# A macaron block on one core: normalisation 3 moves to ScalarE, and four small edits to the routing

## What is computed

```python
x = x + 0.5 * ffn(layernorm(x))
x = x + mixer(layernorm(x))
x = x + 0.5 * ffn(layernorm(x))

# mixer: proj = x @ W_in.T, gate and value halves; depthwise convolution with 5 taps on the value;
# u = sigmoid(gate) * (conv + bias); recurrence h = tanh(a) * h + u over time; res = x + h @ W_out.T;
# the result is layernorm(res) * ln_w + ln_b

# ffn: 32 experts of width 64, 4 chosen for each token, and one shared expert of width 128
scores = sigmoid(tokens @ router_weight.T)
sfc = scores + router_bias
group_scores = top_k(sfc in 4 groups of 8, 2).sum()
keep = the 2 groups with the highest group_scores      # others: sfc := 0
topk_idx = top_k(masked sfc, 4)
topk_w = scores[topk_idx] / (sum + 1e-20) * 2.5
out = sum over chosen of topk_w * (silu(x @ gate.T) * (x @ up.T)) @ down.T  + shared expert
```

## Time and profile before

| | before |
|---|---|
| median of three runs | 779.44 us (778.56 to 781.64) |
| the profiled execution | 780.84 us, span 779.0 us |
| TensorE busy | 737.8 us, 95% |
| VectorE busy | 625.7 us, 80% |
| GpSimd busy | 506.4 us, 65% |
| ScalarE busy | 421.6 us, 54% |
| mean granted clock of TensorE | 0.972 of full speed |

### The profile page before, as it was taken

One profiled execution on the slowest core, in us unless ns is written; L12 is line 12 of the kernel. 1 busy time (PEld: TensorE's weight loads), 2 busy tenths in 40 slices (PEclk: granted clock), 3 DMA queues, 4 the chain that ended last, 5 costly groups with the idle time before them and its releaser, 6 DMA issues. The chain is left out here.

```text
span 779.0 us, 12555 instructions
## 1 busy us (share of the span) xinstructions
PE 737.8 (95%) x3320; PEld 591.0 (76%) x3320; DVE 625.7 (80%) x1719; ACT 421.6 (54%) x777; POOL 506.4 (65%) x716
## 2 busy tenths in 40 slices
PE   6799968899999999999999999999999999988896
PEld 5587756687888788887888788887888788766685
DVE  5887767798789979798789979798789978767853
ACT  4444634365656556565656556565656555544453
POOL 3255754467866777567866787567865786665465
PEclk9799978999999999999999999999999999998999
DMA  7200000000000000000000000000000000000000
GB/s 193 53 0 2 14 0 1 17 11 0 16 1 28 2 1 13 14 14 1 14 0 27 0 1 13 11 17 1 14 0 13 0 0 15 1 0 1 0 14 14
DMA packets 22868, 10.53 MB, mean 14 GB/s; under 512 B 5376, under 2 KB 22816, under 8 KB 22816
## 3 DMA queue, kind: packets, MB, share of 16 engines
q1 hardware_dynamic: 22288, 9.74, 4.5%
q10 hardware_dynamic: 528, 0.26, 0.1%
HBM read 7.90 MB, written 2.10 MB: 13 GB/s over the span
## 5 line engine op out<-in xcount | busy, mean ns | idle before, releaser
L400 POOL TENSOR_TENSOR hid_lo<-hid,hid_hi 128x256 fp32r<-128x256 f32 x544 | 411.3, 778 | 221.6 <-ACT hid_hi L517 220.8
L517 ACT ACTIVATE hid_hi<-hid 128x512 fp32r<-128x512 f32 x272 | 171.1, 629 | 150.1 <-DVE hid L670 125.6
L655 DVE TENSOR_TENSOR weighted<-silu_sb,wb_ps 128x512 f32<-128x512 f32 x256 | 174.4, 681 | 78.2 <-ACT silu_sb L508 44.7
L508 ACT ACTIVATE silu_sb<-gate_ps 128x512 f32<-128x512 f32 x272 | 161.3, 593 | 128.0 <-PE gate_ps L943 126.6
L670 DVE TENSOR_TENSOR hid<-weighted,up_ps 128x512 f32<-128x512 f32 x256 | 174.2, 681 | 13.9 <-DVE weighted L655 1.9
L1006 PE MATMUL down_ps<-hid_lo,wt_hi 128*128 128x512 f32 x272 | 109.1, 401 | 4.2 <-POOL hid_lo L400 4.2
L1003 PE MATMUL down_ps<-hid_hi,wt_hi 128*128 128x512 f32 x272 | 109.8, 404 | 1.5 <-ACT hid_hi L517 1.5
L1004 PE MATMUL down_ps<-hid_hi,wt_lo 128*128 128x512 f32 x272 | 108.6, 399 | 0.0
L941 PE MATMUL gate_ps<-xT_hi,wt_hi 128*128 128x512 f32 x238 | 100.0, 420 | 1.9 <-issue 1.9
L963 PE MATMUL wb_ps<-wT,pick 128*128 128x512 f32 x256 | 100.5, 403 | 0.1
L941 PE MATMUL up_ps<-xT_hi,wt_hi 128*128 128x512 f32 x238 | 95.7, 402 | 2.0 <-DVE hid L670 1.2
(11 more groups left out here) (150 smaller groups left out, 1074.2 us busy)
## 6 DMA issues: line engine op xcount, KB each, us to landing
x_res<-in_L_attn_x SPq DMA_DIRECT2D x8, 256.0 KB, 2.8
out_x<-x SPq DMA_DIRECT2D x8, 256.0 KB, 2.3
x_ln<-in_L_attn_x SPq DMA_DIRECT2D x7, 256.0 KB, 3.0
raw<-in_L_ffn_gate_w SPq DMA_DIRECT2D x4, 256.0 KB, 5.8
raw<-in_L_ffn_up_w SPq DMA_DIRECT2D x4, 256.0 KB, 5.0
raw<-in_L_ffn_down_w SPq DMA_DIRECT2D x4, 256.0 KB, 5.0
x_ln<-in_L_attn_x ACTq DMA_DIRECT2D x1, 256.0 KB, 6.9
raw<-in_L_attn_W_in SPq DMA_DIRECT2D x1, 128.0 KB, 2.7
```

The lines of the kernel that those rows point to most:

```text
L400: last = nc.gpsimd.tensor_tensor(hid_lo[s][:, cols], hid[s][:, cols], hid_hi[s][:, cols].bitcast(F32), ALU.subtract)
L508: nc.scalar.activation(silu_sb[s][:, :], gate_ps[s][:, :], ACT.Silu).then_inc(silu_done, 1)
L517: nc.scalar.activation(hid_hi[s][:, :], hid[s][:, :], ACT.Copy).then_inc(hid_hi_done, 1)
L655: V.tensor_tensor(weighted[s][:, :], silu_sb[s][:, :], wb_ps[j % 2][:, :], ALU.mult)\
```

## The change

Four edits, all in how VectorE's small work is done:

1. The application of normalisation 3 goes from VectorE (four operations, slot 1.5 of a tail unit, slot 10 of a double unit) to ScalarE, which calls `normalise` with `res` as its source, in slot 1 of a tail unit and slot 10 of a double unit, in each behind the silu of that slot and the high part of the tile before. `scaled` and x2 keep their slots.
2. The group differences are made by one operation over all four token groups instead of four.
3. The group mask is an int32 of -1 or 0 (the comparison is multiplied by -1), the masked scores are the bitwise AND of scores and mask, and the addition of 0.0 is gone.
4. `chosen` has a 33rd column, set once to 1e-20, so that the sum over it contains the addition of 1e-20, which is gone. `ROUTE`, the number of counted steps of a routing, goes from 32 to 30.

```diff
-        TAIL = {"meanvar 3": 0, "norm 3": 0, "normalise 3": 1.5, "scale 3": 2, "x2": 3, "stats 4": 3.5,
+        TAIL = {"meanvar 3": 0, "norm 3": 0, "normalise 3": 1, "scale 3": 2, "x2": 3, "stats 4": 3.5,
...
-        ROUTE = 32
+        ROUTE = 30
...
@@ scalar: unit, behind hidden_high(*main, j - 1)
+                    if j == steps.get("normalise 3"):
+                        normalise(3, chain if tail is None else tail, res)
...
@@ vector: route_part
                 if part == 4:
                     st.wait()
-                    for t in range(TT):
-                        last = V.tensor_tensor(gdiff[:, t, :].rearrange("p (g h) -> p g h", g=NG),
-                                               gsum[:, t, :].unsqueeze(1).broadcast_to([P, NG, NG]),
-                                               gsum[:, t, :].unsqueeze(2).broadcast_to([P, NG, NG]), ALU.subtract)
-                    st.done(last)
+                    st.done(V.tensor_tensor(gdiff[:, :, :].rearrange("p t (g h) -> p t g h", g=NG),
+                                            gsum[:, :, :].unsqueeze(2).broadcast_to([P, TT, NG, NG]),
+                                            gsum[:, :, :].unsqueeze(3).broadcast_to([P, TT, NG, NG]),
+                                            ALU.subtract))
...
-                    st.done(V.tensor_scalar(gmask[:, :], grank[:, :], float(GTOP), None, ALU.is_lt))
+                    st.done(V.tensor_scalar(gmask[:, :], grank[:, :], float(GTOP), -1.0, ALU.is_lt, ALU.mult))
                 if part == 6:
                     st.wait()
-                    st.done(V.tensor_tensor(masked0[:, :, :].rearrange("p t (g c) -> p (t g) c", g=NG),
-                                            biased[:, :, :].rearrange("p t (g c) -> p (t g) c", g=NG),
-                                            gmask[:, :].unsqueeze(2).broadcast_to([P, TT * NG, PG]), ALU.mult))
-                    st.wait()
-                    st.done(V.tensor_scalar(masked[:, :, 0:E], masked0[:, :, :], 0.0, None, ALU.add))
+                    st.done(V.tensor_tensor(
+                        masked[:, :, 0:E].bitcast(I32).rearrange("p t (g c) -> p t g c", g=NG),
+                        biased[:, :, :].bitcast(I32).rearrange("p t (g c) -> p t g c", g=NG),
+                        gmask[:, :].rearrange("p (t g) -> p t g", t=TT).unsqueeze(3)
+                        .broadcast_to([P, TT, NG, PG]), ALU.bitwise_and))
...
                     st.done(V.tensor_reduce(wsum[:, :], chosen[:, :, :], AX.X, ALU.add))
-                    st.wait()
-                    st.done(V.tensor_scalar(wsum_e[:, :], wsum[:, :], 1e-20, None, ALU.add))
...
@@ vector: beside
-                if at == steps.get("normalise 3"):
-                    dve.wait_ge(ln_scale[3], tail * 4 + 4)
-                    for t in range(TT):
-                        last = V.tensor_scalar(normed[3][:, t, :], res[:, t, :], rstd[3][:, t:t + 1],
-                                               shift[3][:, t:t + 1], ALU.mult, ALU.add)
-                    last.then_inc(ln_normed[3], 1)
...
@@ vector: setup
+            const.done(V.memset(chosen[:, :, E:E + 1], 1e-20))
```

More of the change, by code:

```diff
@@ L19 @@
 F32R = mybir.dt.float32r
+I32 = mybir.dt.int32
 ALU = mybir.AluOpType
@@ L195, in macaron_kernel @@
         grank = sb("grank", [P, TT * NG])
-        gmask = sb("gmask", [P, TT * NG])
-        masked0 = sb("masked0", [P, TT, E])
+        gmask = sb("gmask", [P, TT * NG], I32)
         masked = sb("masked", [P, TT, E + TOP])
@@ L200, in macaron_kernel @@
         replaced = sb("replaced", [P, TT, E + TOP])
-        chosen = sb("chosen", [P, TT, E])
+        chosen = sb("chosen", [P, TT, E + 1])
         wsum = sb("wsum", [P, TT])
-        wsum_e = sb("wsum_e", [P, TT])
         winv = sb("winv", [P, TT])
@@ L773, in route_part @@
                     st.wait()
-                    st.done(V.scalar_tensor_tensor(chosen[:, :, :], replaced[:, :, 0:E], (FAR + GONE) / 2,
+                    st.done(V.scalar_tensor_tensor(chosen[:, :, 0:E], replaced[:, :, 0:E], (FAR + GONE) / 2,
                                                    score[:, :, :], ALU.is_lt, ALU.mult))
@@ L777, in route_part @@
                     st.done(V.tensor_reduce(wsum[:, :], chosen[:, :, :], AX.X, ALU.add))
-                    st.wait()
-                    st.done(V.tensor_scalar(wsum_e[:, :], wsum[:, :], 1e-20, None, ALU.add))
                 if part == 10:
                     st.wait()
-                    st.done(V.reciprocal(winv[:, :], wsum_e[:, :]))
+                    st.done(V.reciprocal(winv[:, :], wsum[:, :]))
                     st.wait()
-                    st.done(V.scalar_tensor_tensor(weight[:, :, :], chosen[:, :, :], SCALE,
+                    st.done(V.scalar_tensor_tensor(weight[:, :, :], chosen[:, :, 0:E], SCALE,
                                                    winv[:, :].unsqueeze(2).broadcast_to([P, TT, E]),
```

## The result

The changed kernel takes 782.86 us (median of 8 runs, 780.7 to 784.37) where the kernel before takes 779.16 beside it (8 runs, 777.8 to 781.83). The ratio is 1.0037, with a 95% interval of 1.0023 to 1.0052: slower by 3.7 us between the medians, and by 2.9 us (1.8 to 4.1) by the ratio. The forecast was 782.7. The total agrees better than its terms do, as the rest of this text shows.

The account below looks back on a forecast made before the run. TensorE was taken to bound the full tail and chain units, with time to win only where it waits: setup, unit 0, double units. +4.0 +1.1 -0.6 -0.7 -0.5 = +3.3 us on 779.44 gave 782.7, range 777.6 to 785.5.

Parts of the forecast that it names:

- Tail units, +4.0: Six tail units: normalisation 3 on ScalarE delays the chain to hidden tile 3, 5 x 0.70 + 0.5 us; bounds 0 and 6.9.
- the two waits that the prediction summed (0.54 and 0.18): Tail unit: the up product of tile 5 stalls 0.54 us for hidden 3, that of tile 8 another 0.18 for hidden 6.
- The sign given for right: New wait of about 0.5 us before tile 5's up product in each tail, these units at about 42.7 us.
- rival 2: Tail units: x2 held longer beside a low part, so the whole delay shows, 6.9 instead of 4.0, total 785.6; chance 0.12.
- Double units, normalisation 3, +1.1: Two double units: ScalarE needs 1.65 us where VectorE needs 1.11, so `scaled` through to the logits come 0.54 later in each.
- Group differences, -0.6: Last operations of the double units' routing: one operation for four brings hidden tile 15 about 0.3 us earlier in each.
- Setup and unit 0, -1.2: Routing edits: -0.7 us in setup before the `w_tok` transposes, -0.5 in unit 0 at a waiting up product.
- The addition of 1e-20 in the chain units, 0: Chain units: routing savings change nothing, since TensorE waits only 0.13 us in all, behind the recurrence and not behind routing.
- Unit (4,0), 0: One of the six chain units, for all of which the prediction gave no change.
- Tails that hide the activations (778.7): Rival 1: tail units stay at 42.0 us, leaving +1.1 -0.6 -0.7 -0.5 = -0.7, total 778.7; chance 0.20.
- The clock: Rival 3: more waiting in the double units lengthens the half-clock stretch, +1 us per unit, total 784.7; chance 0.07.
- AND at integer type: Rival 4, routing mask: AND dearer than multiplication and addition together, so the small edits' -1.8 us goes, total 784.5; chance 0.06.

## Why the prediction was right, and where not

**What bounds.** Right. Tail and chain units were full (42.00 of 42.00), and the only change that costs something is the one that makes TensorE wait in them.

**Tail units, +4.0.** They took 6.0 and 6.2 in the two pairs of executions. The delays along ScalarE's queue came out as worked out to 0.02 us up to the low part. The step that failed is the one that said that the copy `ffn_sb` "is late as well; its transposes stand before the same up product, so a short wait there lies inside the 0.54". Two instructions of TensorE wait for the copy: the transposes, and the down product of tile 0, which takes its bank over and stands on TensorE ahead of the transposes. The start of that product was in the trace of before, 0.2 us behind the copy's end. The prediction's own times would have given it: the high part of tile 1 at 369.97, the copy 0.52 behind it (367.58 to 368.10 above), 0.58 long and 0.05 for the semaphore, is 371.12 against 370.37, a wait of 0.75. The kernel with normalisation 3 alone has 0.69 there in the same unit, and its unit is 0.93 longer. In after the routing edits add the 0.3 of the looped units: the copy starts 8.55 behind the start of the unit (7.25 before), 1.30 later, less 0.2 of room is 1.1 for 1.2 of length. With that wait TensorE itself is a microsecond late, so that hidden 3 and hidden 6 are in time, and neither of the two waits that the prediction summed (0.54 and 0.18) is there. The sign given for right, a wait of 0.5 us before an up product of tile 5, is absent, and the looped tail units are above 43.1, the sign given for rival 2. Moving x2 changed nothing; moving the activations behind the copy took 3.9 of the 6.0 away.

**Double units, normalisation 3, +1.1.** The step is right in size. In the first double unit of after:

```profile
110.47 1.65 ACT L544 ACTIVATE normed<-res,shift,rstd 128x128 f32<-128x128 f32 x4 [1.34 <-POOL shift L413]
...
112.19 1.29 POOL L431 TENSOR_TENSOR scaled<-normed,lnw_b 128x512 f32<-128x512 f32 x1 [1.76 <-ACT normed L544]
```

GpSimd waits 1.76 between shift and `scaled`, against 1.23 before: 0.53, 0.54 given. In the medians it can't be seen apart from the rest. As a sum the double units went down by 0.8 and 1.2, not up by 0.5. The other traces divide this, one execution each, where executions of one kernel vary by 0.8. Kernels that differ in normalisation 3 alone: 131.9 and 132.8 without, 134.3 with it on ScalarE; 130.1 without, 131.1, 131.2 and 131.6 with it. That is 1.0 to 2.4 more, near the 1.1 given. Kernels that differ in the routing edits alone: 131.9 and 132.8 before, 130.1 with them; 134.3 before, 131.2 and 131.6 with them. That is 1.8 to 3.2 less, where 0.6 was given. So in these traces the routing term of the double units was too small; no run here tells what gives the rest, and the granted clock is part of it (0.87 before and 0.90 and 0.92 after in the first double unit).

**Group differences, -0.6.** The two holds are as given. In the same double unit:

```profile
130.62 0.76 DVE L736 TENSOR_TENSOR gdiff<-gsum 128x64 f32<-128x64 f32 x1
131.41 0.66 DVE L741 TENSOR_TENSOR beats<-gdiff,beat_at 128x64 f32<-128x64 f32 x1
131.99 0.68 DVE L671 TENSOR_TENSOR hid<-weighted,up_ps 128x512 f32<-128x512 f32 x1
...
130.55 1.43 POOL L399 TENSOR_TENSOR hid_lo<-hid,hid_hi 128x256 fp32r<-128x256 f32 x2 [2.60 <-ACT hid_hi L516]
```

The single operation ends about with the first low part, the comparison about with the second, and hidden 15 follows at 131.99, 1.44 behind the start of the low parts; the comparison ended 1.85 behind them before.

**Setup and unit 0, -1.2.** They gave 1.8 to 2.4. The operations cost what was said: in setup the differences take 0.22, the AND 0.29 as the multiplication did, the sum over 33 instead of 32 columns 0.29.

```profile
24.67 0.22 DVE L736 TENSOR_TENSOR gdiff<-gsum 128x64 f32<-128x64 f32 x1
...
25.65 0.29 DVE L751 TENSOR_TENSOR masked<-biased,gmask 128x128 int32<-128x128 int32 x1
...
27.75 0.29 DVE L777 TENSOR_REDUCE wsum<-chosen 128x4 f32<-128x132 f32 x1
...
29.22 0.66 PE L1004 MATMUL side<-ident,w_tok 128*128 128x128 f32 x4 [1.46 <-DVE w_tok L788]
```

The transposes of `w_tok` begin at 29.22 and 29.57 in the two executions of after, at 30.21 and 29.86 in those of before: 0.6 earlier on the mean, 0.7 given. Their wait does not show this, as it depends on when the products ahead ended: 1.46 and 2.72 after, 2.25 and 2.32 before. With the clock as before the two terms together come to 1.3 to 1.6 (the kernel with the routing edits alone), near the 1.2 given. The rest, 0.5 to 0.8, is the clock, which had 0.3 of room in the bounds. From 29 us on it stands at 1.00 in both executions of after, behind a wait of 1.46 and behind one of 2.72, and at 0.50 until 34 us in the kernel with the routing edits alone, behind a wait of 1.60. So the length of this wait does not decide it; what does is open.

**The addition of 1e-20 in the chain units, 0.** Wrong: it was argued that TensorE doesn't wait for the routing there, which is true, and that so the removal does nothing. It moves the operations behind it against GpSimd's low parts, and costs 1.1 us in the four looped tail units.

**Unit (4,0), 0.** The sum over the chain units went down by 1.5 us, all of it in (4,0). Its granted clock from 141 to 150 us is 0.89 in the second execution of before and 1.00 in that of after, behind a pause of TensorE that both have. It comes and goes among the kernels of this study (from 44.7 to 47.2 us), and none of them was made to tell what decides.

**The rivals.** Tails that hide the activations (778.7) fell at once; it is what the kernel with the activations behind the copy does (779.27). The clearly slower case by x2 fell, though its price for the tails, 6.9, is nearer to the truth than 4.0: right in size, by another wait. The clock appeared, on the other side: it is higher in the traces of after in setup, in unit 0 and in (4,0), for no cause that a run here shows; and with a wait of 2.5 us it took 1.7 us a time. AND at integer type costs what the multiplication cost.

**The sum.** Tails 2.1 worse than forecast, setup, unit 0 and (4,0) together some 2.4 better, double units 1.3 to 1.7 better: in the traces the total of 782.86 against 782.7 is errors that cancel, and no proof of the terms. The two halves of the sum, +5.1 for normalisation 3 and -1.8 for the routing, stand up better than the places that they were put together from: measured apart they are +4.8 (3.5 to 6.2) and -2.3 (-1.2 to -3.4). The spans of the two pairs of executions differ by 2.1 and 0.5, less than the medians' 3.7, as both profiled executions of before (780.84 and 782.41 us) lie above its median of 779.16.

**A better kernel.** Group differences in one operation and the mask by AND, with the addition of 1e-20 kept and normalisation 3 left on VectorE, takes 775.53 us, 0.9952 [0.9934, 0.997] of before, and 6.6 us less than the changed kernel by the two ratios. Whether it also beats the kernel with all routing edits (0.9971) is not shown: its tail units are shorter in the traces, 252.1 against 253.5 us, but the intervals of the two ratios overlap.

## What to carry to other kernels

When work is put into an in-order queue, list everything that stands behind it there, and for each of these every waiter, in the order in which the waiters come on their own engine; a copy out of an accumulator bank is waited for by the next product into that bank, not only by whoever reads the copy. Look up how far apart the two ends are in the trace of before: that distance (0.2 us here) is the whole room. And an operation that is removed off the critical path still moves its neighbours: check what starts next to them on an engine that shares the SBUF ports, since 0.1 us decided here between 0.29 and 0.82.

## What the runs showed of the hardware

- Waits of TensorE of 0.46 to 1.11 us, once in each tail unit, left the granted clock at 1.00; one of 2.53 us was followed by 3.4 us at 0.50, so that it cost 1.7 us beyond its own length. Of two waits of nearly the same length, 2.00 and 2.07 us, one left the clock at 1.00 and the other was followed by 0.50.
- A subtraction of 128x128 with two SBUF inputs takes 0.29 us when it starts 0.04 ahead of a GpSimd low part and 0.82 when it starts 0.07 behind one; four normalisations of 128x128 take 1.91 or 2.89 by the low parts that lie over them.
- VectorE idles 1.74 and 1.76 us at the jump back of the loop, though it comes there 0.34 later in the second case; a delay ahead of the pause is not taken up by it.
- Four activations of 128x128 with scale and bias from a tile take 1.65 us, the next activation starting 1.55 after the first; four more of them put what stands behind 1.59 later.
